# Probabilities laid out by pair of token blocks, and one item of eight turns in place of four of four, in a one-core attention and FFN kernel

## What is computed

```python
# x: (32 sequences, 64 tokens, 1024)
c = x @ W.T + b + lora(x)                     # conditioning, per-sequence adapter
q = rope(c @ wq)   # 32 heads of 128
k = rope(c @ wk)   # 8 heads of 128
v = c @ wv         # 8 heads of 128; 4 query heads share one
scores = q k^T * sm_scale, masked causally within each sequence of 64 tokens
out = softmax(scores) @ v
x = x + out @ wo
x = x + ffn(cond2(x))                         # two more projections with routed adapters
```

## Time and profile before

| | before |
|---|---|
| time, median of 3 runs (lowest to highest) | 2785.87 us (2785.77 to 2792.49) |
| the profiled execution | 2785.09 us |
| its span, first to last instruction | 2783.0 us |
| mean granted TensorE clock | 0.990 |
| PE busy | 2698.9 us (97%), 14520 matmul instructions |
| DVE, POOL, ACT busy | 1353.2, 1187.6, 857.3 us |
| HBM traffic | 96 GB/s mean |

### The profile page before, as it was taken

How to read it: one execution, slowest core, us unless ns; L and a number is a source line. 1 busy time by engine, 2 the same in 40 slices (tenths; PEclk the granted TensorE clock), 3 DMA queues, 4 the chain that set the end, 5 groups by cost and what they waited for, 6 DMA issues and landing times.

```text
span 2783.0 us, 37584 instructions
## 1 busy us (share of the span) xinstructions
PE 2698.9 (97%) x14520; PEld 2179.5 (78%) x14520; DVE 1353.2 (49%) x2019; ACT 857.3 (31%) x2089; POOL 1187.6 (43%) x782
## 2 busy tenths in 40 slices
PE   8989999999999999999999999999999999999999
PEld 7877777777777788887877777777777778888877
DVE  3134677667777111124533577777777711112552
ACT  2132344444444211221212334444444421121110
POOL 0035765555655245510304475565555434451020
PEclk9999999999999999999999999999999999999999
DMA  6953122122215333111544312222212443311322
GB/s 220 225 184 113 54 76 77 57 69 72 69 62 188 129 114 109 51 39 55 142 123 122 98 54 74 71 77 76 73 57 69 174 136 106 114 46 38 90 87 68
DMA packets 312498, 268.48 MB, mean 96 GB/s; under 512 B 68730, under 2 KB 283898, under 8 KB 312322
## 3 DMA queue, kind: packets, MB, share of 16 engines
q1 hardware_dynamic: 250722, 210.50, 25.1%
q10 hardware_dynamic: 61600, 55.58, 6.0%
HBM read 201.88 MB, written 64.16 MB: 96 GB/s over the span
## 4 chain that ended last, share of the span: by engine, by line
PE 86%; POOL 6%; ACT 3%; DMA 2%; issue 1%; SPq 1%; DVE 1%; ACTq 0%; POOLq 0%; DVEq 0%
PE prod L673 26%; PE prod L675 25%; PE prod L674 25%; PE turned L919 3%; PE turned L869 2%; POOL s_lo L1496 2%; ACT probs L1254 1%; POOL o_lo L1531 1%; PE turned L667 1%; ACT s_hi L1222 1%; PE turned L902 1%; PE prod L1105 1%; POOL w_lo L1461 1%; POOL w_sum L1521 1%; DMA raw<-in_wo 1%
## 5 line engine op out<-in xcount | busy, mean ns | idle before, releaser
L1461 POOL TENSOR_TENSOR w_lo<-raw,w_hi 128x1024 fp32r<-128x1024 f32 x96 | 239.1, 2492 | 815.2 <-ACT w_hi L1165 815.2
L673 PE MATMUL prod<-o_hi,w_hi 128*128 128x512 f32 x1024 | 402.5, 393 | 12.2 <-POOL o_lo L1531 8.6
L675 PE MATMUL prod<-o_hi,w_lo 128*128 128x512 f32 x1024 | 398.7, 389 | 0.0
L674 PE MATMUL prod<-o_lo,w_hi 128*128 128x512 f32 x1024 | 398.6, 389 | 0.0
L1496 POOL TENSOR_TENSOR s_lo<-w_sum,s_hi 128x512 fp32r<-128x512 f32 x192 | 254.4, 1325 | 259.8 <-ACT s_hi L1222 259.8
L1820 DVE TENSOR_TENSOR x<-prod,x 128x512 f32<-128x512 f32 x128 | 88.5, 692 | 562.3 <-PE prod L675 562.3
L673 PE MATMUL prod<-t_hi,s_hi 128*128 128x512 f32 x768 | 314.2, 409 | 12.2 <-POOL s_lo L1496 12.2
L1165 ACT CAST w_hi<-raw 128x1024 fp32r<-128x1024 f32 x130 | 136.0, 1049 | 609.8 <-PE prod L675 431.5
L675 PE MATMUL prod<-t_hi,s_lo 128*128 128x512 f32 x768 | 301.8, 393 | 0.0
L674 PE MATMUL prod<-t_lo,s_hi 128*128 128x512 f32 x768 | 301.3, 392 | 0.0
L673 PE MATMUL prod<-b_hi,s_hi 128*128 128x512 f32 x576 | 241.4, 419 | 0.0
(11 more groups left out here) (168 smaller groups left out, 5067.2 us busy)
## 6 DMA issues: line engine op xcount, KB each, us to landing
raw_pair<-in_wq SPq DMA_DIRECT2D x64, 512.0 KB, 3.6
o_scratch<-o_out ACTq DMA_DIRECT2D x64, 512.0 KB, 2.9
raw<-in_wo SPq DMA_DIRECT2D x64, 512.0 KB, 3.9
o_raw<-o_scratch SPq DMA_DIRECT2D x64, 512.0 KB, 7.1
raw<-t_scratch SPq DMA_DIRECT2D x50, 512.0 KB, 3.6
t_scratch<-x ACTq DMA_DIRECT2D x17, 512.0 KB, 5.6
x_raw<-in_x SPq DMA_DIRECT2D x16, 512.0 KB, 5.8
xt_scratch<-x_sum SPq DMA_DIRECT2D x16, 512.0 KB, 3.3
```

Source lines behind the costliest of these rows:

```text
L673: pe.matmul(dst, wh, xh, start=start, stop=False)
L674: pe.matmul(dst, wh, xl, start=False, stop=False)
L675: return pe.matmul(dst, wl, xh, start=False, stop=stop)
L1461: pool.tensor_tensor(WL[i % 2][:], RAW[i % 2][:], WH[i % 2][:].bitcast(F32), ALU.subtract).then_inc(w_lo, 1)
```

## The change

Within a tile of four token blocks, two neighbouring blocks are a pair m. The scores are laid out so that a sequence's *block within the pair* (b), and not the head (r), sets the partition half in which its turned probabilities stand. So each sequence's values are needed in one half only:

- `score` writes the same 16 matmuls to other columns of `SCB`; the first of a group waits for `v_in` in place of `s_masked`.
- V's columns are written by DVE in the order (sequence within block, block within pair, token) by `v_cols`: two adds of 256 columns each for every tile in place of one of 512, and no copy around the end (`v_pad` goes).
- `turn_v(gg)` is one item of 8 turns into both PSUM halves, after (01,5); ACT's `v_out` is one copy of 1024 columns. It was 4 items of 4 turns and 4 copies of 512.
- `pv` has 4 matmuls of 64 rows and 256 columns (four heads) in place of 8 of 128 (two heads), alternating between partition halves and PSUM banks as before.
- The items stand elsewhere. `pv(0,0)` goes from after (KV,6) to after (01,0), `turn_p` of unit 3 from (01,0) to (01,1), and the other `pv` from (01,1), (01,3), (01,5) to (01,2), (01,4), (01,6). `turn_p` of unit 2 stays after (KV,5). ACT's `p_out` and `o_out` move with them; the last `o_out` comes behind `v_out` at (01,6).
- For a half's last group, whose items lie in the output projection, places stay.

The core of the diff:

```diff
-                    if v:
+                    if v % 4 == 0:
+                        pe.wait_ge(v_in, gg + 1)
+                    else:
                         pe.wait_ge(s_masked, v)
...
-                                mm = pe.matmul(SCB[s * SEQ:(s + 1) * SEQ, b * P + r * SEQ:b * P + (r + 1) * SEQ],
+                                o = (b // 2) * 2 * P + r * P + (b % 2) * SEQ
+                                mm = pe.matmul(SCB[s * SEQ:(s + 1) * SEQ, o:o + SEQ],
...
-                def turn_v(gg, i):
-                    t, shifted = 1 - i // 2, i % 2
-                    if i == 3:
-                        pe.wait_ge(v_pad, gg + 1)
-                    if i == 0:
-                        if gg:
-                            pe.wait_ge(pt_in, 4 * gg)
-                        pe.wait_ge(quad_in, quad_at(gg * QUADS + QD_KV, A_C21))
-                    else:
-                        pe.wait_ge(v_in, 4 * gg + i)
+                def turn_v(gg):
+                    if gg:
+                        pe.wait_ge(pt_in, 4 * gg)
+                        pe.wait_ge(s_masked, 4 * gg)
+                    pe.wait_ge(quad_in, quad_at(gg * QUADS + QD_KV, A_C21))
                     hold(pe)
-                    for b in range(BPT):
-                        c = (BPT * t + b) * P + (0 if shifted else SEQ)
-                        mm = pe.transpose(TBK[:, b * P:(b + 1) * P], VX[:, c:c + P], ident)
+                    for t in range(TT):
+                        for m in range(2):
+                            for s in range(2):
+                                o = t * NT + (2 * m + s) * P
+                                mm = pe.transpose(TP[0][:, o:o + P], VX[t][:, o - t * NT:o - t * NT + P], ident)
...
-                    for b in range(2):
-                        for s in range(2):
-                            for r in range(2):
-                                rows = slice(r * SEQ, (r + 1) * SEQ)
-                                c = (2 * hb + b) * P + s * SEQ
-                                vv = v_block(2 * (t * BPT + 2 * hb + b) + s, r)
-                                o = b * P + s * SEQ
-                                mm = pe.matmul(view(OB[r], 2)[:, :, o:o + SEQ], VV[rows, vv:vv + HD],
-                                               view(PT[t][rows, :], 2)[:, :, c:c + SEQ], start=True, stop=True)
+                    pt = PT[t][:].rearrange("p (m h s q) -> p m s h q", m=2, h=GQ, s=2)
+                    for s in range(2):
+                        for b in range(2):
+                            rows = slice(b * SEQ, (b + 1) * SEQ)
+                            vv = t * NT + (2 * hb + s) * HD
+                            mm = pe.matmul(view(OB[b], GQ, s * SEQ, (s + 1) * SEQ), VV[rows, vv:vv + HD],
+                                           pt[rows, hb, s], start=True, stop=True)
...
-                                if at_ == (QD_KV, 6):
+                                if at_ == (QD_01, 0):
                                     pv(gg - 1, 0, 0)
-                                if at_ == (QD_01, 0):
+                                if at_ == (QD_01, 1):
                                     turn_p(gg - 1, 1, 1)
-                                if at_ == (QD_01, 1):
+                                if at_ == (QD_01, 2):
                                     pv(gg - 1, 0, 1)
-                                if at_ == (QD_01, 3):
+                                if at_ == (QD_01, 4):
                                     pv(gg - 1, 1, 0)
-                                if at_ == (QD_01, 5):
+                                if at_ == (QD_01, 6):
                                     pv(gg - 1, 1, 1)
-                            if at_ == (QD_01, 6):
-                                turn_v(gg, 0)
-                            if at_ == (QD_23, 0):
-                                turn_v(gg, 1)
+                            if at_ == (QD_01, 5):
+                                turn_v(gg)
...
-                    act.copy(VV[:, c:c + NT], TBK).then_inc(v_in, 1)
+                    act.copy(VV[:], TP[0][:]).then_inc(v_in, 1)
...
-                            add(A_C22, XB, PR_5, XU[:])
-                            add(A_C21, XC, PR_4, XU[:])
-                            dve.wait_ge(quad_in, quad_at(n, A_C22))
-                            dve.tensor_copy(VX[:, 0:SEQ], XB[:, NT - SEQ:NT]).then_inc(v_pad, 1)
+                            for which, i, t in ((A_C22, PR_5, 1), (A_C21, PR_4, 0)):
+                                dve.wait_ge(qprod, q_done(n, i))
+                                for m in range(2):
+                                    xs = slice(m * 2 * P, (m + 1) * 2 * P)
+                                    ins = dve.tensor_tensor(v_cols(t, m), QB[(7 * n + i) % 4][:, xs].rearrange(
+                                        "p (b s k) -> p b s k", b=2, s=2), XU[:, xs].rearrange(
+                                        "p (b s k) -> p b s k", b=2, s=2), ALU.add)
+                                ins.then_inc(quad_in, 1)
```

## The result

| | before | after |
|---|---|---|
| median (lowest to highest) of 6 runs | 2788.98 us (2785.77 to 2792.49) | 2720.58 us (2718.15 to 2724.8) |
| profiled execution; its span | 2785.09; 2783.0 us | 2721.31; 2719.4 us |
| mean granted TensorE clock | 0.990 | 0.995 |

The ratio of the times is 0.9755, 95% interval 0.9743 to 0.9768: faster by 2.45%. The forecast of 2723 us is 2.4 us off, and between the profiled executions, against which the sum was made, the gain is 63.8 us where 62.6 were forecast. The runs before differ with their mean clock (among those measured beside the first experiments, a span of 2781.8 us at 0.990 and one of 2794.5 us at 0.987), so how often the clock falls there varies from run to run.

The account below looks back on a forecast made before the run. PE, holding 86% of the chain, was taken to bound the kernel. From 2785.1 us, -30.3 - 17.3 - 14.7 - 1.2 + 0.9 = -62.6 gave 2723 us; its own range 2712 to 2732, the wider one 2708 to 2750.

Parts of the forecast that it names:

- The wait of `pv(0,0)`: PE's 14 waits for the `probs_t` copy go, with 0.55 us of margin: 14 x 2.17 = -30.3 us.
- The clock: In eleven group windows PE's clock, which fell behind the wait, stays up: 11 x 1.57 = -17.3 us.
- rival A: At `pv(0,0)` the 0.55 us margin is not enough; PE waits about 0.5 us and the clock falls: 2747; 12%.
- Turns of V: On PE's path, one item of eight turns for four of four saves 0.92 us a group, 16 groups: -14.7 us.
- `pv` itself: 64 items with half the records, same columns, overlap kept: 0 taken, bounds 15 us saved to 40 us more.
- Given back at the output projection: At its start PE comes 0.45 us earlier and waits longer for `o_lo`, once in each half: +0.9 us.
- `turn_v` on `v_tok`: On PE, a wait of `turn_v` for the copy before it goes: -1.2 us.
- Hidden parts: DVE's adds cost about 0.5 us more, covered by 1.21 us idle; ACT's copies put nothing on PE's path.
- Rival F: In `QD_01`, ACT's later `o_out(1,0)` delays `pv(1,1)` beyond 2.5 us of slack: near the old time or slower; 6%.
- B: The wait moves with `pv(0,0)`, because it does not hang on the copy: 2770; 5%.
- C: The 256-column `pv` loses the overlap of its partition halves, 40 us more: 2763; 6%.
- E: The clock falls after each item of eight turns of V, 16 x 1.57 = 25 us: 2748; 3%.

Follow-up runs that it names:

- the first experiments: The kernel before with only its items moved as in the change, 2739.68 us, and the changed kernel with items back in old places, 2764.76 us.
- the delayed copies: The changed kernel with two, then four, extra ACT copies in front of the copy that `pv(0,0)` needs: 2728.05 us, then 2744.1 us.
- the spread alone: The kernel before with its items moved as in the change, but with the old `turn_v` and `pv` layout: 2739.68 us, ratio 0.9815.
- the run with one half alone: The changed kernel with every `pv` matmul reading partitions 0 to 63 of probabilities and values: 2776.66 us in one run.
- layout alone: The changed kernel with its items back in the old places and the eight turns of V behind (01,6): 2764.76 us, ratio 0.9907.

## Why the prediction was right, step by step

**The wait of `pv(0,0)`** (-30.3): right in size and cause. It is gone in the change and in each kernel with that one item moved, and back nearly in full (29.7 us) when it is put back. The margin was forecast at 0.55 us from one group; it is 0.53 in most groups, but down to 0.32 in four. Product (01,0), which now runs in the hole, found its inputs ready.

**The clock** (-17.3): right where it was priced: all twelve windows between waits are at 1.00 after. (The prediction counts eleven windows like the longer one. There are nine of them, and the other two of the eleven falls lie behind the last wait of either half, so the sum stands.) Over the whole run the term was a little too large: the time lost to the clock is 1.0% of 2783.0, 27.8 us, before and 0.5% of 2719.4, 13.6 us, after, or 14.2 less (these means are rounded to 0.1%; the clock's own records in the traces say 27.9 and 13.7). The rest is not in the windows: away from the 14 waits, at the starts of stages above all, where PE waits with and without the change, the clock fell three times more in the trace after than in that before. That is 9.1 us lost before and 13.7 after; in the other kernels of this study whose clock did not fall at these waits the whole loss is 10.2 to 14.4 us, so I take the difference for scatter. The pricing in rival A, a fall behind any wait, was wrong, as the delayed copies show.

**Turns of V** (-14.7): right. Group windows give it apart from the clock: the changed kernel less the one with the spread alone is 71.38 - 70.33 = 1.05 us a group, of which 0.92 was forecast for the turns and 4 x 0.03 is `pv`. The windows after are 0.27 us shorter than the 70.6 forecast. `pv` gives 0.11 of it. Another 0.07 is the wait itself, which costs more than its listed idle time: that is counted from the end of the last record, 0.39 us behind its start, where an item that waits for nothing starts at 0.32. The last 0.09 us have no cause shown.

**`pv` itself** (0, bounds -15 to +40): 0.028 us an item, 1.8 us in all. The value taken was right, its reasoning in part: the overlap of the halves is real (the run with one half alone), but it doesn't hang on strict alternation, and the bound of -15 rested on all of the 0.23 us being a cost of the records, when it is the edge of the form, which the change keeps.

**Given back at the output projection** (+0.9): waits on `o_lo` went from 8.6 to 10.2 us, so +1.6: the term was sized too small by 0.7, with two more short waits than before.

**`turn_v` on `v_tok`** (-1.2): gone. It was also the one crowding that the spread without the layout made worse.

**Not forecast:** waits on `s_lo` at the start of the two attention stages are 8.4 us for 12.2. In the other runs of this study, with the same work there, they lie between 8.3 and 11.9, so this is scatter of one execution and no effect of the change. Sum of the terms as measured: -30.3 - 14.2 - 14.7 - 1.8 - 1.2 + 1.6 - 3.8 = -64.4, against 63.6 us of span. That the total came within 1.2 us is in part luck: against the forecast the clock gave 3.1 us less and `o_lo` took 0.7 more, while the scatter of `s_lo` gave 3.8 and `pv` 1.8.

**Hidden parts.** DVE's four adds (x4 in its timeline after) and ACT's late `o_out`:

```profile
730.04 1.40 DVE L1777 TENSOR_TENSOR v_rows<-prod,quad_b 128x256 f32<-128x256 f32 x4
732.90 0.20 DVE L1727 RECIPROCAL row_rcp<-row_sum 128x8 f32<-128x8 f32 x1 [1.47 <-ACT probs L1245]
```

```profile
752.52 1.07 ACT L1268 COPY o_out<-turned 128x512 f32<-128x512 f32 x2
```

```profile
756.08 0.70 PE L916 MATMUL turned<-probs_t,v_tok 64*128 64x256 f32 x4
```

The adds take 1.40 us, less than the two adds and the copy before (753.13 to 754.79, 1.66 us), where 0.5 us more was allowed, and DVE idles 1.47 us behind them (1.21 before). Rival F's copy is over at 753.59 and its `pv(1,1)` starts at 756.08: 2.49 us of slack, as forecast (2.5). No run tested what happens when it is used up.

**The rivals.** A, B, C, D, E and F did not come about. E's eight turns in a row leave the clock at 1.00 behind all 16 items; the rule of the page named there does not make itself felt in this mix.

## What to carry to other kernels

When an in-order engine waits at one spot for a copy that is late by less than one unit of its other work, move that one consumer behind one more unit, and read the margin off the timeline first: here one item moved was worth 48.5 us of span, and the holes' own 30 us were under two thirds of it, since the clock fell behind most of them. Price small matmuls by the columns that each partition half streams and by the edges of the 64-row form, not by their number, keep the two halves close to each other in PE's list, and issue such items together where PSUM allows it. Operands laid out so that each is needed in one partition half only gained here about what the turns saved cost, 0.11 us each.

## What the runs showed of the hardware

- The clock fell behind 11 of 14 waits of 2.14 to 2.18 us (before) and 8 of 14 of 2.1 to 2.3 us (layout alone), and behind none of 28 between 0.4 and 1.65 us (delayed copies), all waits of `pv(0,0)` for the same copy, the last 28 one product later in PE's list. A fall costs a group about 1.6 us. This is no limit for other places: in the trace before, the clock fell at 139.9 us, in the first stage, between a wait of 1.63 us that ended at 138.2 and one of 0.30 us that ended at 140.6.
- fp32 matmuls of 64 rows in different partition halves overlap fully when they alternate or have four records of the other half ahead (1.06 and 1.07 us an item) and in part with eight ahead (1.64, where alternating takes 1.09). In one half they don't overlap at all (1.92).
- An item of 64-row matmuls between 128-row ones costs about 0.4 us beyond its columns (0.41 and 0.45 against the 128-row form, 0.38 by issuing two together), whatever the number of matmuls: 0.03 us for eight records more.
